# A transformer block on one core: the first FFNs' indirect transfers wait for the one two in front, and all of a scatter goes ahead of the next batch's places

## The chip, the cores and the metric

The kernel runs on one core of a Trainium2 chip. A core has five engines that run their own instruction streams and meet through semaphores: PE (matmul, with a half called PEld that loads weights), DVE (vector), ACT (scalar, activation), POOL (GpSimd) and SP (which here only issues plain DMAs). Plain DMAs are issued by SP; indirect ones, where each of 128 rows goes to or comes from a row number held in SBUF, are issued by POOL. The metric is the device time of one execution in microseconds (us), as the median of several.

## The reference

All is float32; x is 4 batches of 1024 tokens of 128 channels.

```python
x = x + attn_a(layernorm(x))     # gated attention in groups of 32 plus a linear part, 256 inner channels
x = x + ffn(layernorm(x))        # mixture of experts: 8 experts, each token goes to its best 2
x = x + attn_b(layernorm(x))     # 16 heads of 64, softmax over the queries
x = x + ffn(layernorm(x))        # the same experts again

def ffn(x):                      # per batch: T tokens, E = 8, capacity = T / E * 1.25 = 160
    probs = softmax(x @ Wr); topk_probs, topk_experts = top_k(probs, 2)
    pos = place of the token in its expert's queue   # a running count over the tokens
    keep = pos < capacity
    buf[expert, pos] += x * keep                     # scatter to 8 x 160 slots
    y = relu(buf @ W1 + b1) @ W2 + b2                # per expert, hidden 512
    out = sum over k of y[expert, pos] * keep * topk_probs   # gather from the slots
```

## The kernel before

The four batches ("rows" in the code, 0 to 3) pass through attn_a one after the other (`a_tensor`, `a_scalar`, `a_vector`). The FFN's routing of a batch is woven into the row after next or so: while row 2 is worked on, the first FFN batch is scattered, and so on. FFN batches are numbered m = 1, 2, 3 here (the fourth runs inside attn_b). For each m the chain is: logits, choice of two experts on DVE (`choose_vector`), `positions` on PE (a running count by small bfloat16 matmuls with a triangle and with ones), `kept_vector` on DVE, then the "places": arithmetic that turns positions into row numbers of the slot array `xslots` in HBM. For m = 1 and 2 POOL computes the places (`place_gpsimd`), for m = 3 DVE (`place_vector`) and POOL copies the result to `row_s`. Then POOL issues the scatter: 16 indirect transfers (2 choices x 8 tiles of 128 tokens, 512 bytes a row), one after the other in its own stream.

When the transfers go is set by `hold`, a wait on POOL. In the scatters of m = 1 and 2 each transfer or pair waits for an event of the attention on PE (`scatter_in_attention`: a_vproj, a_lktr, a_sq, a_sl, a_kv, a_o, a_out; `scatter_in_next`: a_xproj, a_gproj), and the last three of batch 1's sixteen stand in the row after. The scatter of m = 3 and the gather of batch 1's answers wait, two transfers at a time, for an expert's first product (`beside_expert`, f_h). The landings all count on one semaphore, f_sc, 256 for a scatter. No transfer waits for another.

SP loads the slots back, 640 KB at a time, once the 16 transfers have landed: to `slots_sb` for m = 1, to `slots2` (in `vact`) for m = 2, to `slots3` (in `state`) for m = 3. Between the last two it stores the answers of batch 1 to `yslots`. PE's experts run as `experts_tensor` for m = 1, 2, 3: for each of 8 experts an up product (L412) and a down product (L446), eight blocks each of 1.09 us; `positions` for m = 3 stands behind the third down product of m = 1. The gather of batch 1 (16 indirect transfers, `yg`) feeds DVE's `first_answers_vector`, in four quarters; then come the statistics of the new x, a Newton iteration and the normalized `xhat`, which PE transposes (L498) at the end of `experts_tensor` for m = 3 and which all of attn_b starts from.

Behind that, from about 214 us on, attn_b fills PE, and the later FFN work is done in its side; its indirect transfers are each held for a step of the attention (`paced`).

Of the kernel before, what the change touches and what calls it, by code (L numbers as in the profile page):

```python
# [19 lines left out]
U32 = mybir.dt.uint32  # L20
I32 = mybir.dt.int32
ALU = mybir.AluOpType
# [3 lines left out]
P = 128  # L26
# [23 lines left out]
def bass_hybrid(nc, x, wv, bv, wg, win, wout, bout, cols_a, wr, w1, b1, w2, b2, wqkv, bqk, bvv, wl, bl, out):  # L50
    with ExitStack() as keep:
# [81 lines left out]
        f_plc = sem("f_plc")  # L133
# [133 lines left out]
        def route_norm_scalar(a, k):  # L267
            a.wait_ge(lf_rstd, k + 1)
            if k == 0:
                a.wait_ge(zeroed, ZEROED)  # L270
            elif k == 2:
                a.wait_ge(f_sc, 256)
# [81 lines left out]
        row_s = sb("row_s", [P, 2, T], U32, stack=stage_f)  # L354
        slots_sb = sb("slots_sb", [P, ST, P], stack=stage_f)
# [68 lines left out]
        def experts_tensor(pe, m, beside, residual=None, turned=TR, begun=False, following=None):  # L424

            def up(e):
# [6 lines left out]
                if e == 5 and m == 1:  # L433
                    pe.wait_ge(f_kept, 3)
# [181 lines left out]

        def place_gpsimd(p, step, m):
# [15 lines left out]
            if m > 1:  # L633
                p.wait_ge(f_sc, 256 * (m - 1))
            nc.gpsimd.tensor_copy(row_s[:], skip[:]).then_inc(f_idx, 1)

        def place_vector(v, step, m):
# [11 lines left out]
            nc.vector.tensor_tensor(skip[:], rowf[:], skip[:], ALU.add).then_inc(f_plc, 1)  # L649

        def first_answers_vector(v, step):
# [4 lines left out]
            for q in range(4):  # L656
                v.wait_ge(f_gq[q], 64)
# [8 lines left out]
        def scatter(p, m, tiles):  # L666

            for c in tiles:
                k, t = c // T, c % T
                nc.gpsimd.indirect_dma_start(out=xslots[:, :], out_offset=bass.IndirectOffsetOnAxis(ap=row_s[:, k, t:t + 1], axis=0),  # L670
                                             in_=route_rows(m - 1)[:, t, :], in_offset=None,
                                             bounds_check=B * SLOTS - 1, oob_is_err=False).then_inc(f_sc, 16)

        def scatter_in_attention(p, m, next_row=None):

            r = m + 2
            hold(p, f_idx, m + 1)
            hold(p, a_vproj, 4 * r + 4)
            scatter(p, m, [0])
            hold(p, a_lktr, 2 * r + 2)  # L680
            scatter(p, m, [1])
            hold(p, a_sq, 2 * r + 2)
            scatter(p, m, [2])
            for h in range(2):
                hold(p, a_sl, 2 * r + h + 1)
                scatter(p, m, [3 + h])
            for k in range(2):
                hold(p, a_kv, 4 * r + 2 * k + 1)
                scatter(p, m, [5 + k])
            for k in range(4):  # L690
# [1509 lines left out]
```

## Time and profile before

| | |
|---|---|
| three timed runs | 1462.74, 1464.06, 1464.46 us (median 1464.06) |
| span of the profiled execution, first to last instruction | 1486.9 us |
| the profiled execution's own time beside its span | not reported; it is the span and what lies around it |
| busy: PE, PEld, DVE, ACT, POOL | 1437.6, 1023.7, 1065.3, 917.8, 280.4 us |
| the 16 transfers each of three scatters and one gather | between 79.9 and 201.4 us of the span |

In the rows below a time is in us from the start of the span. In the rows of a timeline the columns are the start, the length, the engine, the line of the kernel, the operation with its operands (written, then read) and how many are merged into the row; the bracket gives the engine's idle time before it and what ended it. "remote" and "another core or an unknown queue" mean that the profile has no instruction to name; "issue" means that it shows nothing that was waited for.

### The profile page before, as it was taken

Reading aid. Unit: us, or ns where it says so; the run is one execution under the profiler, and the core shown is the slowest. Engines: PE = TensorE matmul, PEld = TensorE weight load, DVE = VectorE, ACT = ScalarE, POOL = GpSimd, SP = SyncE. Lnnn points to the kernel's source line nnn. Section 1 sums busy time; section 2 is a strip of 40 time slices with the busy share of each in tenths; the row PEclk is TensorE's granted clock in tenths of the full one; section 3 lists DMA queues with packets and bytes.
Section 4 is the critical chain, followed back from the end, with each engine's and each line's share of the span. In section 5 each row is a group of like instructions: output and inputs, shape, how many; then the busy total and the mean of one; then the engine's idle time right before and its main releaser. Section 6 shows DMA issues by size and latency. Waiting matters only on the chain.

```text
span 1486.9 us, 43341 instructions
## 1 busy us (share of the span) xinstructions
PE 1437.6 (97%) x18426; PEld 1023.7 (69%) x18426; DVE 1065.3 (72%) x2172; ACT 917.8 (62%) x1727; POOL 280.4 (19%) x325
## 2 busy tenths in 40 slices
PE   7999789999999999999999999999999999999996
PEld 6988774566677675667777756577777565677486
DVE  6884037888666678886766788876666887787754
ACT  5774466666666666566666666666666666666542
POOL 4164613013210012130000120400001214000055
PEclk9999999999999999999999999999999999999999
DMA  8501221001110011010000110110101101101002
GB/s 223 196 20 53 68 65 39 22 23 46 30 29 16 16 42 32 23 48 16 17 16 16 41 32 22 35 33 17 30 16 39 32 23 34 34 16 30 1 19 58
DMA packets 44464, 58.30 MB, mean 39 GB/s; under 512 B 8231, under 2 KB 32656, under 8 KB 44144
## 3 DMA queue, kind: packets, MB, share of 16 engines
q1 hardware_dynamic: 35120, 38.27, 9.4%
q0 software_dynamic: 9152, 17.26, 4.4%
q8 instruction: 147, 2.41, 0.7%
q14 instruction: 45, 0.37, 0.1%
HBM read 22.14 MB, written 19.32 MB: 28 GB/s over the span
## 4 chain that ended last, share of the span: by engine, by line
PE 87%; DVE 5%; ACT 3%; issue 2%; another core or an unknown queue 2%; DMA 0%; DVEq 0%; ACTq 0%
PE bank L1153 29%; PE bank L1166 28%; PE bank L1076 6%; PE bank L1081 4%; PE bank L1090 4%; PE bank L412 2%; PE bank L446 2%; PE bank L1308 2%; PE bank L1304 2%; DVE nmx L1188 1%; PE bank L1265 1%; ACT hT L542 1%; PE bank L830 1%; DVE stats L1349 1%
## 5 line engine op out<-in xcount | busy, mean ns | idle before, releaser
L1197 ACT ACTIVATE prob<-bank,nmx 128x1024 f32<-128x1024 f32 x512 | 570.2, 1114 | 420.3 <-DVE nmx L1188 408.5
L1188 DVE TENSOR_REDUCE nmx<-bank 128x1 f32<-128x1024 f32 x512 | 626.2, 1223 | 200.2 <-PE bank L1153 182.3
L1166 PE MATMUL bank<-prob,vsc 64*64 64x512 f32 x4096 | 644.9, 590 | 1.9 <-DVE ctxT L1215 1.4
L1153 PE MATMUL bank<-q,k 64*64 64x512 f32 x2048 | 527.6, 591 | 3.1 <-ACT prob L1197 1.9
L1153 PE MATMUL bank<-q,ks 64*64 64x512 f32 x2048 | 526.3, 590 | 0.0
L1166 PEld LDWEIGHTS bank<-prob,vsc 64*64 64x64 f32 x4096 | 237.3, 133 | 119.4 <-issue 47.1
L1076 PE MATMUL bank<-xT,wqkv_sb 64*64 64x256 f32 (+1 forms) x1560 | 211.7, 434 | 0.0
L1153 PEld LDWEIGHTS bank<-q,ks 64*64 64x64 f32 x2048 | 139.1, 133 | 75.9 <-issue 21.0
L1760 POOL DMA_INDIRECT yg<-yslots,row_ring x64 | 64.9, 1014 | 609.2 <-PE bank L1153 579.8
L1153 PEld LDWEIGHTS bank<-q,k 64*64 64x64 f32 x2048 | 135.3, 133 | 37.6 <-issue 8.6
L1076 PEld LDWEIGHTS bank<-xT,wqkv_sb 64*64 64x64 f32 x1560 | 92.2, 133 | 86.6 <-issue 36.5
L1081 PEld LDWEIGHTS bank<-wqkv_sb,xT 64*64 64x64 f32 x1984 | 105.5, 133 | 34.7 <-issue 16.6
L1090 PEld LDWEIGHTS bank<-wl_sb,ctxT 64*64 64x64 f32 x1984 | 108.1, 133 | 28.2 <-issue 8.9
L1081 PE MATMUL bank<-wqkv_sb,xT 64*64 64x128 f32 x1984 | 118.8, 270 | 0.0
L1090 PE MATMUL bank<-wl_sb,ctxT 64*64 64x128 f32 x1984 | 117.4, 270 | 0.3 <-issue 0.3
L1771 POOL DMA_INDIRECT xslots<-xhat_r,row_s x64 | 62.3, 974 | 206.0 <-PE bank L1153 182.7
L1197 ACT ACTIVATION_READ_ACCUMULATOR prob<-bank,nmx 128x1 f32 x512 | 98.7, 193 | 0.0
L1207 DVE TENSOR_TENSOR vsc<-v,zinv 128x128 f32<-128x128 f32 x256 | 74.8, 292 | 8.8
L1132 DVE TENSOR_TENSOR v<-bank,bvv_sb 128x512 f32<-128x512 f32 x64 | 44.2, 691 | 41.5 <-PE bank L1081 41.2
L542 ACT ACTIVATE hT<-bank,b_sb 128x160 f32<-128x160 f32 x160 | 50.0, 411 | 34.7 <-PE bank L412 20.9
L1304 PE MATMUL bank<-xsT,w_sb 64*64 64x160 f32 x768 | 68.2, 296 | 0.0
L1119 DVE TENSOR_TENSOR xres<-bank,xres 128x512 f32<-128x512 f32 x64 | 44.0, 688 | 23.7 <-PE bank L1090 22.0
(270 smaller groups left out, 1628.6 us busy)
## 6 DMA issues: line engine op xcount, KB each, us to landing
ks<-k SPq DMA_DIRECT2D x62, 256.0 KB
yslots<-slots_sb SPq DMA_DIRECT2D x7, 640.0 KB, 3.6
slots_sb<-xslots SPq DMA_DIRECT2D x5, 640.0 KB, 4.5
xslots<-xhat_r POOLq DMA_DIRECT2D x5, 512.0 KB, 7.0
yslots<-xhat_r POOLq DMA_DIRECT2D x5, 512.0 KB, 12.3
w_sb<-in_w SPq DMA_DIRECT2D x1, 2048.0 KB, 9.2
wqkv_sb<-in_wqkv SPq DMA_DIRECT2D x1, 2048.0 KB, 19.0
xslots<-xhat_r,row_s POOLq DMA_INDIRECT x112
```

What stands on the lines that cost most here:

```text
L542: ins = nc.scalar.activation(hT[:, e % deep(m), c, :], bank[:, UP_BANK[e % deep(m)] + c // 2, cols(c % 2, CAP)], ACT.Relu, bias=b1_sb[:, e ...
L1076: ins = nc.tensor.matmul(bank[rows(h), PJ[0] + t, 0:n], wqkv_sb[rows(r), row, c + h * HD:c + (h + 1) * HD], xT_c[rows(r), k % 2 * HALF + t ...
L1081: ins = nc.tensor.matmul(bank[rows(h), bk, cols(i)], xT_c[rows(r), cols(8 * (k - 4) + 2 * t + h, HD)], wqkv_sb[rows(r), row, WV:WV + P], s ...
L1090: ins = nc.tensor.matmul(bank[rows(h), bk, cols(i)], ctxT[pi % 2][rows(r), cols(8 * k + 2 * t + h, HD)], wl_sb[rows(r), pi % PAIRS, :], st ...
L1153: ins = nc.tensor.matmul(bank[rows(c), SC[h][n], :], kk[r, cols(2 * j + c, HD)], qst[pi % 2][r, cols(n, HALF)], start=True, stop=True)
L1166: ins = nc.tensor.matmul(bank[rows(h), CX[n], :], vsc[s][rows(r), rows(h)], prob[g % 3][h][rows(r), cols(n, HALF)], start=(j == 0 and firs ...
L1188: nc.vector.tensor_reduce(nmx[:, 2 * s + h:2 * s + h + 1], bank[:, SC[h][0]:SC[h][0] + 2, :], mybir.AxisListType.XY, ALU.max, negate=True) ...
L1197: nc.scalar.activation(prob[g % 3][h][:].rearrange("p (n c) -> p n c", c=HALF), bank[:, SC[h][0]:SC[h][0] + 2, :], ACT.Exp, bias=nmx[:, 2 ...
L1207: nc.vector.tensor_tensor(vsc[s][:].rearrange("p (h c) -> p h c", c=HD), vst[pi % 2][:, j, :].rearrange("p (h c) -> p h c", c=HD), zinv[:, ...
L1304: ins = nc.tensor.matmul(bank[rows(h), bk, cols(q, CAP)], w1_sb[rows(r), e, cols(4 * (i % 2) + 2 * q + h, HD)], xsT[rows(r), cols(e, CAP)] ...
L1760: nc.gpsimd.indirect_dma_start(out=yg[:, k, t, :], out_offset=None, in_=yslots[:, :], in_offset=bass.IndirectOffsetOnAxis(ap=row_ring[:, f ...
L1771: nc.gpsimd.indirect_dma_start(out=xslots[:, :], out_offset=bass.IndirectOffsetOnAxis(ap=row_s[:, k, t:t + 1], axis=0), in_=xhat_r[:, t, : ...
```

## The change

- In the three scatters and in the gather of batch 1, every transfer from the third on waits until the one two in front of it has landed. For that the semaphores f_sc and f_gq are split into an even and an odd one for each batch or quarter. The waits on events of the attention and of the experts are gone.
- All sixteen transfers of batch 1 go before the places of batch 2, with the bias of row 3 between the eighth and the ninth; before, three of them stood in the next row. The places of batch 2 go to a buffer of their own, `row_s2`, and no longer wait for the landing of batch 1.
- `positions` for m = 3 stands in front of the experts of m = 1, not behind their third down product. DVE writes the third batch's row numbers to `row_s` itself; POOL's copy is gone.

```diff
@@ semaphores
-        f_plc = sem("f_plc")
...
-        f_sc, f_ld, f_st, f_comb = (sem(n) for n in ("f_sc", "f_ld", "f_st", "f_comb"))
+        f_sc = {m: [sem(f"f_sc{m}{i}") for i in range(2)] for m in (1, 2, 3)}
+        f_ld, f_st, f_comb = (sem(n) for n in ("f_ld", "f_st", "f_comb"))
...
-        f_gq = [sem(f"f_gq{q}") for q in range(4)]
+        f_gq = [[sem(f"f_gq{q}{i}") for i in range(2)] for q in range(4)]
@@ experts_tensor, up(e)
-                if e == 5 and m == 1:
+                if e == 2 and m == 1:
                     pe.wait_ge(f_kept, 3)
@@ first_batch_tensor, beside(e)
-                if e == 3:
-                    positions(pe, 3, POS_F)
                 if e == E - 1:
-                    pe.wait_ge(f_kept, 3)
                     slots_ahead_tensor(pe, 2, slots2, AHEAD[:2])
@@ place_gpsimd
+        def rows_to(m):
+            return row_s2 if m == 2 else row_s
...
-            if m > 1:
-                p.wait_ge(f_sc, 256 * (m - 1))
-            nc.gpsimd.tensor_copy(row_s[:], skip[:]).then_inc(f_idx, 1)
+            nc.gpsimd.tensor_copy(rows_to(m)[:], skip[:]).then_inc(f_idx, 1)
@@ place_vector
-            nc.vector.tensor_tensor(skip[:], rowf[:], skip[:], ALU.add).then_inc(f_plc, 1)
+            for done in f_sc[1]:
+                v.wait_ge(done, 128)
+            nc.vector.tensor_tensor(rows_to(m)[:], rowf[:], skip[:], ALU.add).then_inc(f_idx, 1)
@@ scatter
                 k, t = c // T, c % T
-                nc.gpsimd.indirect_dma_start(out=xslots[:, :], out_offset=bass.IndirectOffsetOnAxis(ap=row_s[:, k, t:t + 1], axis=0),
+                if c > 1:
+                    hold(p, f_sc[m][c % 2], 16 * (c // 2))
+                nc.gpsimd.indirect_dma_start(out=xslots[:, :], out_offset=bass.IndirectOffsetOnAxis(ap=rows_to(m)[:, k, t:t + 1], axis=0),
                                              in_=route_rows(m - 1)[:, t, :], in_offset=None,
-                                             bounds_check=B * SLOTS - 1, oob_is_err=False).then_inc(f_sc, 16)
+                                             bounds_check=B * SLOTS - 1, oob_is_err=False).then_inc(f_sc[m][c % 2], 16)
-        def scatter_in_attention(p, m, next_row=None):
...
-        def scatter_in_next(p, m):
...
-        def beside_expert(p, i):
...
+        FIRST = 8
@@ gather
-                    beside_expert(p, 11 + 2 * q + k)
                     for t in (2 * q, 2 * q + 1):
+                        n = 4 * q + 2 * k + t % 2
+                        if n > 1:
+                            hold(p, f_gq[(n - 2) // 4][n % 2], 16 * ((n - 2) % 4 // 2 + 1))
...
-                                                     bounds_check=B * SLOTS - 1, oob_is_err=False).then_inc(f_gq[q], 16)
+                                                     bounds_check=B * SLOTS - 1, oob_is_err=False).then_inc(f_gq[q][t % 2], 16)
@@ the block of gpsimd
             place_gpsimd(p, step, 1)
-            scatter_in_attention(p, 1, 3)
-            scatter_in_next(p, 1)
+            hold(p, f_idx, 2)
+            scatter(p, 1, range(FIRST))
+            bias_gpsimd(p, 3)
+            scatter(p, 1, range(FIRST, 2 * T))
             place_gpsimd(p, step, 2)
-            scatter_in_attention(p, 2)
-            scatter(p, 2, [13, 14, 15])
-            p.wait_ge(f_plc, 1)
-            p.wait_ge(f_sc, 256 * 2)
-            nc.gpsimd.tensor_copy(row_s[:], skip[:]).then_inc(f_idx, 1)
+            hold(p, f_idx, 3)
+            scatter(p, 2, range(2 * T))
             hold(p, f_idx, 4)
-            for i in range(8):
-                beside_expert(p, 3 + i)
-                scatter(p, 3, [2 * i, 2 * i + 1])
+            scatter(p, 3, range(2 * T))
             gather(p, step, 1, 0)
@@ the block of tensor
             pe.wait_ge(f_sub, 4)
+            positions(pe, 3, POS_F)
             experts_tensor(pe, 1, first_batch_tensor(pe), (a_res, 10), following=slots2)
```

Beside these, the waits on f_sc in `route_norm_scalar`, `load_slots`, `f_norm_vector` and SP's block become waits on the two semaphores of the batch (128 each).

The POOL stream around the end of the second scatter and the start of the third, before (row_s and row_s2 are the row numbers, xhat_r and xhat_r1 the rows sent):

```order
L670 DMA xslots<-xhat_r1,row_s 5120x128 [waits a_o] x4
L670 DMA xslots<-xhat_r1,row_s 5120x128 [waits a_out] x2
L670 DMA xslots<-xhat_r1,row_s 5120x128 x3
L2065 CAST row_s<-skip 128x16 [waits f_sc,f_plc]
L670 DMA xslots<-xhat_r,row_s 5120x128 [waits f_idx,f_h]
L670 DMA xslots<-xhat_r,row_s 5120x128
```

and now:

```order
L675 DMA xslots<-xhat_r1,row_s2 5120x128 [waits f_sc20]
L675 DMA xslots<-xhat_r1,row_s2 5120x128 [waits f_sc21]
L675 DMA xslots<-xhat_r,row_s 5120x128 [waits f_idx]
L675 DMA xslots<-xhat_r,row_s 5120x128
L675 DMA xslots<-xhat_r,row_s 5120x128 [waits f_sc30]
L675 DMA xslots<-xhat_r,row_s 5120x128 [waits f_sc31]
```

The waits on PE's events (a_o, a_out, f_h) have given way to waits on landings of the same scatter, and POOL's copy between the two scatters is gone.

The PE stream at the end of row 3 and the start of the experts, before (chosen holds the choice, xsT the slots, hT the hidden values):

```order
L852 MATMUL bank<-wout_sb,gateT 128x128 x15
L412 MATMUL bank<-xsT,w1_sb 128x160 [waits f_xs,f_sub,load_f]
L412 MATMUL bank<-xsT,w1_sb 128x160 [waits a_res]
L446 MATMUL bank<-hT,w2_sb 128x160 [waits f_ya,f_ha]
L379 MATMUL bank<-chosen,before 128x64 [waits f_m]
L412 MATMUL bank<-xsT,w1_sb 128x160 [waits f_ha,f_kept]
```

and now:

```order
L824 MATMUL bank<-wout_sb,gateT 128x128 x15
L381 MATMUL bank<-chosen,before 128x64 [waits f_m,f_sub,load_f]
L383 MATMUL bank<-chosen,ones 128x56
L414 MATMUL bank<-xsT,w1_sb 128x160 [waits f_xs]
L414 MATMUL bank<-xsT,w1_sb 128x160 [waits f_kept,a_res]
```

The count of positions has moved ahead of the first expert, and the wait for f_kept from the sixth expert's up product to the third's.

## Rows read from the trace of the kernel before

**Rows 1.** The page: who holds the chain that ended last

```profile
PE 87%; DVE 5%; ACT 3%; issue 2%; another core or an unknown queue 2%; DMA 0%; DVEq 0%; ACTq 0%
```

**Rows 2.** The chain of waits, 108 to 215 us: start, length, what

```profile
119.87 6.31 another core or an unknown queue
...
154.43 3.92 another core or an unknown queue
...
161.37 2.67 another core or an unknown queue
...
179.47 3.62 another core or an unknown queue
...
184.43 3.54 issue
```

**Rows 3.** Timeline of ACT and of PE, 110 to 225 us

```profile
126.20 1.08 ACT L331 ACTIVATE xT_r<-bank 128x512 f32<-128x512 f32 x2 [6.33 <-remote]
...
120.23 1.04 PE L313 MATMUL bank<-ident,xhat_r 128*128 128x128 f32 x8
...
127.43 2.64 PE L370 MATMUL bank<-wr_sb,xT_r 128*128 128x8 f32 x16 [0.25 <-ACT xT_r L331]
```

**Rows 4.** Timeline of POOL, 0 to 330 us

```profile
79.94 1.12 POOL L670 DMA_INDIRECT xslots<-xhat_r,row_s  x1 [1.04 <-issue]
...
148.55 0.20 POOL L2065 CAST row_s<-skip 128x16 uint32<-128x16 f32 x1 [5.54 <-DVE skip L649]
149.70 0.98 POOL L670 DMA_INDIRECT xslots<-xhat_r,row_s  x1 [0.95 <-POOL row_s L2065]
150.99 0.97 POOL L670 DMA_INDIRECT xslots<-xhat_r,row_s  x1 [0.30 <-issue]
...
171.39 0.97 POOL L670 DMA_INDIRECT xslots<-xhat_r,row_s  x1 [0.30 <-issue]
...
178.49 1.00 POOL L721 DMA_INDIRECT yg<-yslots,row_g  x1 [0.30 <-issue]
...
200.44 1.00 POOL L721 DMA_INDIRECT yg<-yslots,row_g  x1 [0.30 <-issue]
```

**Rows 5.** Windows: stretch, its length, busy time, then the granted clock (PEclk)

```profile
128.50:135.20 6.70, 6.70 (x33) 6.70 (x33) 3.78 (x17) 1.81 (x5) 1.69 (x2) 0.50 0.10 32
...
186.50:193.20 6.70, 5.23 (x20) 5.23 (x21) 1.49 (x6) 2.64 (x7) 0.79 (x1) 0.50 0.08 20
400.00:560.00 160.00, 160.00 (x2322) 115.34 (x2318) 110.21 (x169) 102.97 (x191) 14.93 (x15) 1.00 0.10 25
```

**Rows 6.** Timeline of ACT near the end

```profile
1475.17 0.88 ACT L1868 ACTIVATE answers<-bank,slot_owner 128x128 fp32r<-128x128 f32 x3 [9.69 <-remote]
```

**Rows 7.** Timeline of PE in row 2

```profile
89.03 0.82 PE L313 MATMUL bank<-ident,xhat_r 128*128 128x128 f32 x6
...
94.52 1.85 PE L370 MATMUL bank<-wr_sb,xT_r 128*128 128x8 f32 x16
```

**Rows 8.** Timeline of DVE: it takes up the gathered rows, then xhat

```profile
181.09 1.26 DVE L654 SCALAR_TENSOR_TENSOR xres<-yg,wtok_ring,xres 128x128 f32<-128x128 f32 x4 [32.61 <-DMA yg<-yslots,row_g]
...
203.42 1.26 DVE L654 SCALAR_TENSOR_TENSOR xres<-yg,wtok_ring,xres 128x128 f32<-128x128 f32 x4 [3.62 <-DMA yg<-yslots,row_g]
...
208.54 2.14 DVE L1374 TENSOR_SCALAR xhat<-xres,meanvar,rstd 128x128 f32<-128x128 f32 x8
```

**Rows 9.** SP's queue: the store of answers and the load of state

```profile
167.20 0.36 SPq L732 DMA_DIRECT2D yslots<-slots_sb  x1
173.63 0.36 SPq L1995 DMA_DIRECT2D state<-xslots  x1
```

**Rows 10.** Timeline of PE: the experts' wait for kept; the transposes of xhat

```profile
146.67 1.35 PE L412 MATMUL bank<-xsT,w_sb 128*128 128x160 f32 x8 [0.45 <-DVE tmp L615]
...
211.95 1.04 PE L498 MATMUL bank<-ident,xhat 128*128 128x128 f32 x8
```

**Rows 11.** Groups of POOL's instructions by line: the scatters inside attn_b

```profile
L1771 POOL DMA_INDIRECT xslots<-xhat_r,row_s x64 | 62.3, 974 | 206.0 <-PE bank L1153 182.7 <-issue 23.2
```

More of the change, by code:

```diff
@@ L271, in route_norm_scalar @@
             elif k == 2:
-                a.wait_ge(f_sc, 256)
+                for done in f_sc[1]:
+                    a.wait_ge(done, 128)
             for half in range(2):
@@ L354, in bass_hybrid @@
         row_s = sb("row_s", [P, 2, T], U32, stack=stage_f)
+        row_s2 = sb("row_s2", [P, 2, T], U32, stack=stage_f)
         slots_sb = sb("slots_sb", [P, ST, P], stack=stage_f)
@@ L648, in place_vector @@
                                               kept[:].rearrange("p k t -> p (k t)"), ALU.mult))
-            nc.vector.tensor_tensor(skip[:], rowf[:], skip[:], ALU.add).then_inc(f_plc, 1)
+            for done in f_sc[1]:
+                v.wait_ge(done, 128)
+            nc.vector.tensor_tensor(rows_to(m)[:], rowf[:], skip[:], ALU.add).then_inc(f_idx, 1)
         def first_answers_vector(v, step):
@@ L656, in first_answers_vector @@
             for q in range(4):
-                v.wait_ge(f_gq[q], 64)
+                for done in f_gq[q]:
+                    v.wait_ge(done, 32)
                 for k in range(2):
@@ L669, in scatter @@
                 k, t = c // T, c % T
-                nc.gpsimd.indirect_dma_start(out=xslots[:, :], out_offset=bass.IndirectOffsetOnAxis(ap=row_s[:, k, t:t + 1], axis=0),
+                if c > 1:
+                    hold(p, f_sc[m][c % 2], 16 * (c // 2))
+                nc.gpsimd.indirect_dma_start(out=xslots[:, :], out_offset=bass.IndirectOffsetOnAxis(ap=rows_to(m)[:, k, t:t + 1], axis=0),
                                              in_=route_rows(m - 1)[:, t, :], in_offset=None,
-                                             bounds_check=B * SLOTS - 1, oob_is_err=False).then_inc(f_sc, 16)
-        def scatter_in_attention(p, m, next_row=None):
[L676 to L690, printed above, removed]
-                hold(p, a_o, 4 * r + k + 1)
-                scatter(p, m, [7 + k])
-                if k == 1 and next_row is not None:
-                    bias_gpsimd(p, next_row)
-            for h in range(2):
-                hold(p, a_out, 2 * r + h + 1)
-                scatter(p, m, [11 + h])
-        def scatter_in_next(p, m):
-            r = m + 3
-            hold(p, a_xproj, 2 * r + 2)
-            scatter(p, m, [13])
-            for k in range(2):
-                hold(p, a_gproj, 4 * r + 2 * k + 2)
-                scatter(p, m, [14 + k])
-        def beside_expert(p, i):
-            hold(p, f_h, E + i + 1)
+                                             bounds_check=B * SLOTS - 1, oob_is_err=False).then_inc(f_sc[m][c % 2], 16)
+        FIRST = 8
         def gather(p, step, m, b):
@@ L1415, in f_norm_vector @@
                 else:
-                    v.wait_ge(f_sc, 256 * (B - 1))
+                    for done in f_sc[B - 1]:
+                        v.wait_ge(done, 128)
                 xhat_vector(v, c0, fb, xhat_r, piece - 5, g_xhat)
@@ L1992, in _ @@
                     store_slots(sp, 1, 0)
-                hold(sp, f_sc, 256 * m)
+                for done in f_sc[m]:
+                    hold(sp, done, 128)
                 hold(sp, f_ld, 16 * m)
```

3 lines of the change are left out of this document (2 added, 1 removed).

## The prediction

> **What bounds the kernel now.** I read the page first: the chain that ended last is 87% PE, so most of the 1,486.9 us is matmul time that nothing in this change touches [rows 1]. The change lies between 79.9 and 204 us, on POOL's indirect transfers, so I went on to the chain of waits in 108 to 215 us. It is PE and ACT work, broken by five stretches in which the chain can name no instruction: 6.31, 3.92, 2.67, 3.62 and 3.54 us, 20.1 us in all [rows 2]. I call them freezes. They are not waits for data. ACT's copy of xT_r starts at 126.20 after 6.33 us of idle, although the transposes that it reads began at 120.23 and take 1.04 us [rows 3]. Then I set POOL's rows beside them [rows 4]: every freeze falls into a run of indirect transfers issued back to back, one each 1.28 us (scatter) or 1.30 us (gather). After them PE runs at half clock: granted 0.50 from 128.5 to 135.2 and from 186.5 to 193.2 [rows 5], which is 1.2 of 2.4 GHz, each time after PE had had gaps.
>
> Are the freezes there when nobody records? The span is 1,486.9 us; what lies around it only adds to it; the three timed runs have a median of 1,464.06 us. So the recorded execution is at least 22.8 us longer than an ordinary one. From 214 to 1,400 us there is no room for that: PE works nearly without a gap at full clock. What I can take out as freeze is about 17 us up to 212 us (worked out below) and some 8 us at the end, where the same kind of freeze holds ACT for a good part of 9.69 us [rows 6]. 1,486.9 - 25 = 1,462, next to the median. The likeliest reading is that the timed runs hardly have these freezes. So my sum is made on a clock of the profile without them, and carried over to the median as a difference.
>
> **That clock.** Row 2 of the attention turns its first block at 89.03, row 3 at 120.23, 31.20 later. In row 2 the logits start at 94.52, behind 0.87 us of transposes that row 3 lacks; so row 3's belong at 124.85 and stand at 127.43: +2.6. The 6.7 us at half clock that follow leave 3.3 us of work undone: 5.9 us in all [rows 3, 5, 7]. Next, xsT is late by about 2.9 us at 158.37 and yT by 2.7 at 164.06 [rows 2]: 11.5 us by the store at 167.20, which belongs at 155.7 [rows 9]. From there to the transposes of xhat PE has 30 blocks of eight matmuls at 1.09 (32.7), 2.2 of transposes and some 2 of short waits: 37, so PE is done at 192.7, not 211.95 [rows 10].
>
> **The path before.** The third FFN's scatter starts at 149.70 - 5.9 = 143.8. Sixteen at 1.28: the last starts at 162.9 and ends at 163.9. The load of state that waits for it comes 2.24 after its start, at 165.1, and makes PE wait less than a us (193.5) [rows 9]. The copy of row_g and 0.95 of start-up put the first gather at 165.0; with 15 x 1.30 the last starts at 184.5. DVE takes it up 2.98 later and ends xhat 7.26 after that (203.42 to 208.54 + 2.14) [rows 4, 8]: 194.8. So POOL's chain already ends about a us behind PE. That is the stage's bound.
>
> **The change part by part.**
> 1. *The wait for the one two in front.* Nothing but the next transfers stands behind it on POOL. Three kinds of row price it. A scatter is seen landed 2.24 us after its start (171.39 to the load at 173.63). A gather is seen landed 2.60 us after the start of the fourth of the first quarter (178.49 to 181.09) and 2.98 after that of the last (200.44 to 203.42) [rows 4, 8, 9]. And from the end of what an indirect transfer waited for to its own start there are 0.95 us (row_s at 148.55 + 0.20, transfer at 149.70) [rows 4]. In the present stream that 0.95 lies beside the transfer before; behind a landing it lies bare. So a pair takes 2.24 + 0.95 = 3.2 us, or 1.60 each, for scatters and 2.60 + 0.95 = 3.55, or 1.78 each, for gathers. Ends: nothing (1.28 and 1.30 kept, if most of the 0.95 still overlaps), and 1.97 for gathers (2.98 throughout). I take 1.60 and 1.78, as the rows are from this very stage.
> 2. *Scatter before places.* Batch 1: eight transfers from 79.94 [rows 4], the last at 90.8; then the bias of row 3, which waits for ACT's xhat of that row and so ends near 94.2; eight more from 94.4, the last ends at 106.3, some 2.6 us before the present end. The places of batch 2 take 4.7 us and end at 111.0; POOL began them without idle before, and f_kept, which comes from DVE at the head of row 3, is there by then as well. Batch 2's sixteen from 112.0: the last starts at 135.7. Row 3 no longer has its holds (a_o, a_out), so POOL is not late through PE any more, only through its own pace.
> 3. *Positions in front of the experts, DVE writes row_s itself.* PE ends the output products at 131.4 (137.3 - 5.9), so positions end near 131.9 and DVE's residual, which stands ahead of kept, near 132.6; then 0.5, and the 2.1 us from f_kept (146.6) to row_s (148.75): f_idx at 135.2, against 142.9 before (148.75 - 5.9) [rows 4, 10]. It removes a PE wait of 0.45 us [rows 10] and POOL's copy. The eight small matmuls (0.35 us) only move. The third expert's up waits for f_kept, which comes about when PE gets there.
> 4. *Batch 3 and the gather.* POOL is free at 137.0, so most of the 7.7 us won by part 3 is lost to the pace of batch 2. Sixteen at 1.60: the last starts at 160.6; copy and start-up: first gather at 162.8 (the store has landed near 159.7); the last starts 1.3 + 24.9 later, at 188.9; + 2.98 + 7.26 = 199.0. The load of state now comes early enough and gives PE its 0.8 back, unused.
> 5. *Semaphores split by parity, more holds on SP, DVE, ACT:* waits long met; cost nothing.
>
> Sum: 199.0 - 194.8 = +4.2 us at the transposes of xhat, on which all of the attention behind depends, and which nothing later gives back (PE is the bound from there on). PE would stand still for some 5 us there; the half clock behind earlier gaps [rows 5] could add 1 to 3 us, shorter landings without the recorder take as much off. I say +4: 1,468 us.
>
> The Trainium skill, DMA: Bandwidth & Descriptors, section "Anatomy of one DMA — SWDGE (gpsimd) path", puts about 2.0 us of fixed cost on a transfer, most of it completion, while many descriptors can be emitted before that costs anything. This speaks against the change: what was hidden behind the next issue becomes the pace. My rows have 2.24 to 2.98, so the trace agrees in kind and is higher in size. By the page's 2.0 the pace would be an estimated 1.48 for both, the last gather would start near 182, and POOL would be no later than before; that is the second rival's result.
>
> **The rivals.**
> - *The freezes are real in every execution and the pace ends them.* The price is what the profile shows: xhat's transposes move from 211.95 to about 199 to 200, -12 to -13 us, so 1,451. It decides from the point at which more than about 7 us of the 17 exist in a timed run. For it: they are large, all lie in back-to-back runs, and the far looser stream of the attention behind (64 scatters with 206 us of idle before them [rows 11]) shows none. Against it: 1,464 leaves no room for them. A remainder of 5 to 10 us would give 1,455 to 1,461.
> - *The pace costs less than the start gains.* With 1.50 and 1.70 the same sum ends at 195.9 (+1.1); with 1.28 and 1.30 batch 3 starts at 136.2, xhat is done by 187, and PE's 192.7 is the bound (-2). So 1,462 to 1,466. For it: all latencies were read while the recorder ran; against it: they come from two kinds of transfer and three places that agree within 0.8 us.
> - *The change doesn't do what it says:* two in flight is what a landing of 2.25 at a step of 1.28 keeps anyway, so real freezes would stay, beside the cost of the pace: 1,466 to 1,470.
>
> **How the numbers follow.** The kernel's own runs differ by 1.7 us; about 0.2% (2.9 us) is what can be told from no change. Forecast (+2.9 to +8) 0.43; pace for nothing (-2.9 to +2.9) 0.28; freezes real and ended 0.25, half of it with the full gain; real and kept 0.04. Slower 0.46, same 0.30, faster 0.24. The forecast's own range is 1,466 to 1,472; the high end is gathers at 1.97 (+7) and a little half clock. Downwards I reach to 1,453, so that only the full gain is left out.
>
> **What would show it.** In the changed kernel's profile: scatters 1.5 to 1.65 us apart and gathers 1.7 to 1.85 (1.3 would prove the second rival's pace, over 1.9 the high end); the last gather near 189 us; DVE's last sum 2.6 to 3.0 us behind it; PE waiting at the transposes of xhat for DVE, not for slots. The freezes may well be gone from the record, and its span some 12 us shorter: that alone doesn't show a gain in the timed runs, and I would be right only if they still come out longer. I am wrong if the timed runs follow the record.

## The result and the profile after

The changed kernel took 1479.32 us in the median of four runs (1477.55 to 1480.85), the kernel before 1463.4 us beside it (1461.79 to 1464.46): a ratio of 1.0108 [1.0094, 1.0123]. It is 15.9 us slower; +4 was forecast, with 1,472 us as the high end. The direction was right, the size wrong by a factor of four.

The profiled execution of the changed kernel took 1478.24 us with a span of 1476.2, so 2.0 us lie around the span. The page's line on the chain, and PE's longest waits between 60 and 230 us (line <- what ended the wait: us in total, times, longest), answer to [rows 1, 10]:

```profile
PE 85%; issue 4%; DMA 3%; POOL 3%; DVE 3%; ACT 1%; POOLq 0%; DVEq 0%; ACTq 0%
```

```profile
PE bank L497 <- DVE xhat L1346: 11.4, 1, 11.4
PE bank L403 <- DMA state<-xslots: 4.8, 1, 4.8
```

POOL and DMA now have a share of the chain, and PE stands still for 11.4 us before the transposes of xhat. The load of state, which was to come early enough, makes it wait 4.8. Timeline of POOL from the end of batch 2's scatter into the gather, answering to [rows 4]:

```profile
137.99 0.97 POOL L675 DMA_INDIRECT xslots<-xhat_r,row_s  x1 [0.57 <-issue]
139.26 0.97 POOL L675 DMA_INDIRECT xslots<-xhat_r,row_s  x1 [0.31 <-issue]
140.54 0.97 POOL L675 DMA_INDIRECT xslots<-xhat_r,row_s  x1 [0.30 <-issue]
142.43 0.97 POOL L675 DMA_INDIRECT xslots<-xhat_r,row_s  x1 [0.91 <-DMA xslots<-xhat_r,row_s]
147.17 0.97 POOL L675 DMA_INDIRECT xslots<-xhat_r,row_s  x1 [3.77 <-DMA xslots<-xhat_r,row_s]
148.45 0.98 POOL L675 DMA_INDIRECT xslots<-xhat_r,row_s  x1 [0.30 <-issue]
...
166.56 0.98 POOL L675 DMA_INDIRECT xslots<-xhat_r,row_s  x1 [0.31 <-issue]
...
168.67 1.08 POOL L692 DMA_INDIRECT yg<-yslots,row_g  x1 [0.93 <-POOL row_g L683]
170.06 1.01 POOL L692 DMA_INDIRECT yg<-yslots,row_g  x1 [0.30 <-issue]
174.32 1.00 POOL L692 DMA_INDIRECT yg<-yslots,row_g  x1 [3.25 <-DMA yg<-yslots,row_g]
...
177.76 1.00 POOL L692 DMA_INDIRECT yg<-yslots,row_g  x1 [1.14 <-DMA yg<-yslots,row_g]
...
186.48 1.00 POOL L692 DMA_INDIRECT yg<-yslots,row_g  x1 [2.89 <-DMA yg<-yslots,row_g]
...
198.93 0.99 POOL L692 DMA_INDIRECT yg<-yslots,row_g  x1 [0.61 <-issue]
```

An undisturbed pair of scatters costs 1.28 + 1.80 = 3.08 us, a pair of gathers from 1.30 + 2.1 = 3.4 up to 3.66 (3.5 in the mean of four). That is 1.54 and 1.70 to 1.83 a transfer, where the forecast has 1.60 and 1.78: the price of an undisturbed pair was right. Between such pairs stand waits of 3.77, 3.25 and 2.89 us. The chain of waits has the landings behind them (start of the transfer, time until its landing released POOL, what), and the timeline of SP's queue shows what moved beside them:

```profile
113.02 3.76 DMA xslots<-xhat_r,row_s
...
140.54 5.79 DMA xslots<-xhat_r,row_s
...
154.88 3.43 DMA xslots<-xhat_r,row_s
...
168.67 4.81 DMA yg<-yslots,row_g
...
174.32 2.60 DMA yg<-yslots,row_g
177.76 2.70 DMA yg<-yslots,row_g
181.30 4.34 DMA yg<-yslots,row_g
```

```profile
140.24 0.38 SPq L1969 DMA_DIRECT2D vact<-xslots  x1
154.32 0.36 SPq L704 DMA_DIRECT2D yslots<-slots_sb  x1
168.85 0.36 SPq L1969 DMA_DIRECT2D state<-xslots  x1
181.64 0.36 SPq L704 DMA_DIRECT2D yslots<-slots_sb  x1
```

Four of the landings are late, 5.8 and 3.4 us for scatters, whose median here is 2.2, and 4.8 and 4.3 for gathers, against 2.6 and 2.7 between them. Each belongs to a transfer issued within 0.6 us of a plain transfer of 640 KB. A fifth late landing, 3.76 us from 113.02 on, makes POOL wait 2.28 us at 117.62 with no plain transfer beside it: the load of slots_sb had been issued at 107.47 and had landed by 111.9.

The wait on PE ends with DVE's xhat, from its timeline:

```profile
207.22 2.14 DVE L1346 TENSOR_SCALAR xhat<-xres,meanvar,rstd 128x128 f32<-128x128 f32 x8
```

Behind that long wait PE works at half clock (granted 0.50). In a table of windows (stretch, length, busy time of PE, PEld, DVE, ACT and POOL, then the granted clock):

```profile
208.40:214.00 5.60, 5.52 (x22) 4.10 (x24) 2.22 (x6) 2.66 (x5) 0.00 (x0) 0.50 0.00 0
```

For comparison a second record of the kernel before is wanted, because its first has the freezes. It was taken later (below) with a span of 1462.4 us, and it has no freeze. Its timelines of POOL, DVE and PE answer to [rows 4, 8, 10]:

```profile
82.30 1.12 POOL L670 DMA_INDIRECT xslots<-xhat_r,row_s  x1 [1.04 <-issue]
...
164.43 0.97 POOL L670 DMA_INDIRECT xslots<-xhat_r,row_s  x1 [0.30 <-issue]
...
186.24 1.00 POOL L721 DMA_INDIRECT yg<-yslots,row_g  x1 [0.30 <-issue]
```

```profile
194.33 2.14 DVE L1374 TENSOR_SCALAR xhat<-xres,meanvar,rstd 128x128 f32<-128x128 f32 x8
```

```profile
195.59 2.05 PE L498 MATMUL bank<-ident,xhat 128*128 128x128 f32 x8 [2.21 <-DVE xhat L1374]
```

The first scatter starts at 80.1 us in some executions and near 82 in others, of the old kernel and the new alike; so the stage is best measured from there. From the first scatter's start to the end of xhat the kernel before takes 196.47 - 82.30 = 114.2 us (forecast: 194.8 - 79.94 = 114.9). The changed kernel takes 209.36 - 80.17 = 129.2 (forecast 119.1). That is +15.0, and the median time rose by 15.9. The two recorded executions themselves differ by 14.0 us: 15.0 in this stage, 2.1 less ahead of the first scatter (80.17 for 82.30), and some 1.4 more right behind xhat. Nothing behind gives anything back.

### The profile page after: what moved, and what is told of

Its sections match the earlier page's. It is cut to its first block, busy times and chain, and to the rows that moved or that the text cites. A ratio compares the mean times of both kernels' runs of the same rounds, so it can differ in the third digit from the quotient of the medians.

```text
span 1476.2 us, 43358 instructions
## 1 busy us (share of the span) xinstructions
PE 1428.9 (97%) x18426; PEld 1026.2 (70%) x18426; DVE 1068.6 (72%) x2172; ACT 918.7 (62%) x1727; POOL 280.6 (19%) x324
## 4 chain that ended last, share of the span: by engine, by line
PE 85%; issue 4%; DMA 3%; POOL 3%; DVE 3%; ACT 1%; POOLq 0%; DVEq 0%; ACTq 0%
PE bank L1125 30%; PE bank L1138 29%; PE bank L1048 6%; PE bank L1053 4%; PE bank L1062 3%; PE bank L1280 2%; POOL xslots L675 2%; PE bank L1276 2%; DMA yg<-yslots,row_g 2%; PE bank L1237 1%; DMA xslots<-xhat_r,row_s 1%; PE bank L414 1%; PE bank L448 1%; DVE nmx L1160 1%; PE bank L1909 1%
## 5 line engine op out<-in xcount | busy, mean ns | idle before, releaser
L1138 PEld LDWEIGHTS bank<-prob,vsc 64*64 64x64 f32 x4096 | 240.4, 133 | 116.5 <-issue 41.6
L1280 PE MATMUL bank<-hT,w_sb 64*64 64x160 f32 x768 | 60.2, 296 | 0.0
```

What stands on the lines that cost most here:

```text
L1138: ins = nc.tensor.matmul(bank[rows(h), CX[n], :], vsc[s][rows(r), rows(h)], prob[g % 3][h][rows(r), cols(n, HALF)], start=(j == 0 and firs ...
L1280: ins = nc.tensor.matmul(bank[rows(h), bk, 0:CAP], w2_sb[rows(r), i, q, rows(h)], hT[rows(r), i % 2, q, :], start=first and q == 0, stop=n ...
```

## The experiments

"Free" below is the changed kernel without the waits for landings, so only the new order. Ratios are to the kernel before, run beside each.

**1. The pace taken apart.** Free leaves out both of these lines, gather free only the second, scatter free only the first:

```diff
-                if c > 1:
-                    hold(p, f_sc[m][c % 2], 16 * (c // 2))
...
-                        if n > 1:
-                            hold(p, f_gq[(n - 2) // 4][n % 2], 16 * ((n - 2) % 4 // 2 + 1))
```

> The changed kernel without the waits for landings (three scatters and the gather issue freely); order, positions and semaphores as changed. Theory (the pace is the whole cost, and it is the bound through POOL's chain): 1461 to 1464 us, 0 to 2 us under the kernel before, since scatter 3 starts earlier and PE becomes the bound. Rival 1 (the new order costs by itself): stays above 1470. Rival 2 (recorded freezes are real in timed runs): its record shows freezes again and the timed run is then longer than the changed kernel's 1479. The theory expects the freezes back in the record, span 1480 or more, with a timed run near 1463.

> The changed kernel with the pace in the scatters alone; the gather issues freely. Theory: the gather takes 15 x 1.30 instead of 30.3 us, so xhat is ready some 10.5 us earlier (near 198.5): 1467 to 1470 us, still some 5 us over before, for the load of state comes late (PE waits 4.8 us for it). Rival (the order costs): as the changed kernel, 1479, less little.

> The changed kernel with the pace in the gather alone; scatters issue freely. Theory: scatter 3 starts near 136 and ends by 156, so the gather starts when the store has landed, 9 to 10 us earlier: 1468 to 1471 us. Together with the other half (gather free) the two savings need not add up, as PE is the bound behind some 192 us. Rival (the order costs): 1479.

Measured: free 1458.5 us, 0.9969 [0.9957, 0.9981]; pace in the scatters only 1466.95, 1.0024 [1.0015, 1.0033]; pace in the gather only 1468.0, 1.0037 [1.0024, 1.0051]. So the new order alone is 4.7 us faster than before, where I expected 0 to 2, and the pace costs 20.8 us on top (21.6 when both were run again side by side): 8.4 for scatters and 9.5 for gathers alone. Why the medians of the two don't add up to the whole is not shown. PE's slack in the free version, which either half uses up first, is small: xhat is ready at 188.8 and PE comes to it at 190.13. The records have it larger for each half: the stretch from the first scatter's start to the last gather's is 98.2 us in the free version, 109.9 and 109.3 with the pace in the scatters or the gather, and 118.8 with both, and the recorded executions took 11.6, 11.0 and 21.9 us more than free's. Of free, the timeline of POOL, and of PE at the transposes:

```profile
130.84 0.98 POOL L673 DMA_INDIRECT xslots<-xhat_r,row_s  x1 [0.30 <-issue]
135.46 0.98 POOL L673 DMA_INDIRECT xslots<-xhat_r,row_s  x1 [3.65 <-DVE row_s L651]
...
154.73 0.98 POOL L673 DMA_INDIRECT xslots<-xhat_r,row_s  x1 [0.30 <-issue]
158.75 1.09 POOL L688 DMA_INDIRECT yg<-yslots,row_g  x1 [2.83 <-DMA yslots<-slots_sb]
...
178.38 0.99 POOL L688 DMA_INDIRECT yg<-yslots,row_g  x1 [0.30 <-issue]
```

```profile
190.13 1.04 PE L497 MATMUL bank<-ident,xhat 128*128 128x128 f32 x8
```

POOL is led by data (row_s at 135.46, the store at 158.75), and PE reaches the transposes without a wait. My expectation that the freezes would be back in this record fell: it shows none, although every scatter and the gather are issued back to back once their data is there. That a back-to-back stream is enough for them is refuted.

The free version's record has late landings too, although nothing waits for them. Its gathers issued at 174.48, 175.78 and 177.08 land after 4.5, 4.8 and 3.7 us, beside the store of batch 2's answers (issued at 174.85); so the pace doesn't make these landings late, it only waits for them. But three of its scatters, at 111.51, 124.41 and 140.60, land after 3.7, 3.9 and 3.9 us with no plain transfer under way. Plain transfers are therefore not the only source of late landings; the other one is open.

**2. How far in front.** Three kernels wait for the landing of the one directly in front, three in front and four in front (the last two with four semaphores instead of two). The wait of the scatters in the first of them:

```diff
-                if c > 1:
-                    hold(p, f_sc[m][c % 2], 16 * (c // 2))
+                if c > 0:
+                    hold(p, f_sc[m][(c - 1) % 2], 16 * ((c + 1) // 2))
```

> The changed kernel, but each indirect transfer waits for the landing of the one directly in front. My theory: a transfer in this form costs its landing plus the bare start-up behind a wait: scatters 2.3 + 0.9 = 3.2 us apart (1.6 in the changed kernel), gathers 2.7 + 0.9 = 3.6 to 3.8 (1.85 to 1.9). 48 scatters x 1.55 + 16 gathers x 1.85 is about 104 us more before xhat, nothing of it hidden: 1,565 to 1,600 us. Rival, the start-up lies beside the landing in front: 2.3 and 2.7 us apart, so 0.75 x 48 + 0.85 x 16 = 50 us more, 1,525 to 1,535. Rival, the cost of the pace sits in what the holds do to other engines and not in the landings: far below 1,520.

> The changed kernel, but each transfer waits for the landing of the one three in front. My theory (a landing and 0.9 us of start-up have to fit into n steps of issue): 2.3 + 0.9 = 3.2 is under 3 x 1.28 = 3.84, and 2.7 + 0.9 = 3.6 under 3.90, so the pace costs nothing but beside the plain transfers of 640 KB, about 1 to 3 us at each of the four in the way, of which 3.7 us are hidden behind PE: 1,458 to 1,462. Rival, any wait for a landing costs its start-up of 0.9 us bare: 0.3 us per transfer and 1,468 to 1,474.

> The changed kernel, but every transfer waits for the one four in front instead of two (four semaphores for each scatter). Theory: four transfers cover 4 x 1.28 = 5.1 us, more than a landing of 2.2 to 3 plus 0.9, so the wait binds only beside a plain 640 KB transfer (landings up to 5 us): within 2 us of the kernel with no waits, 1462 to 1466. Rival (a wait on POOL costs by itself, landed or not): near 1479. If recorded freezes come from a deep queue, they are here as in the kernel with no waits.

Measured: one 1568.91 us, 1.0722 [1.0706, 1.0739]; (two: 1479.32); three 1460.05, 0.9976 [0.9966, 0.9987]; four 1457.84, 0.9959 [0.9945, 0.9972]. "Four" came out 4 us below its range of 1,462 to 1,466, which was built on too slow a forecast for free, but within the 2 us of free that the expectation named; "one" and "three" lie in theirs. With "one", POOL's timeline shows the whole price of a landing with the start-up bare:

```profile
154.42 0.98 POOL L675 DMA_INDIRECT xslots<-xhat_r,row_s  x1 [1.97 <-DMA xslots<-xhat_r,row_s]
157.37 0.97 POOL L675 DMA_INDIRECT xslots<-xhat_r,row_s  x1 [1.98 <-DMA xslots<-xhat_r,row_s]
...
281.94 0.99 POOL L692 DMA_INDIRECT yg<-yslots,row_g  x1 [2.66 <-DMA yg<-yslots,row_g]
285.63 0.99 POOL L692 DMA_INDIRECT yg<-yslots,row_g  x1 [2.69 <-DMA yg<-yslots,row_g]
```

Undisturbed, that is 2.95 to 3.1 us a scatter and 3.4 to 3.7 a gather. So the form of the cost holds: landing plus start-up has to fit into n steps of issue. Two steps (2.56 to 2.60) are too short. Three (3.84, 3.90) are long enough except at late landings (3.6 to 5.8 us in that record), which lengthen the stage by 4.6 us over free but the time by only 1.5. Four cost nothing. Four in front and free can't be told apart; they are the best versions run, some 5 us below the kernel before.

**3. The pace in the old order.** The kernel before with the same two waits for landings, its holds on PE and ACT kept.

> The kernel before with its order of work, but every scatter and gather waits for the landing of the one two in front. My theory: the pace costs the same in either order wherever transfers stood back to back, that is in batch 3's scatter and in the gather: about 0.35 x 16 + 1.9 for the plain store beside it = 7.5 us, and the 9.5 us that the gather's pace alone cost; so about 17 us over the kernel before less 0 to 3 us of slack: 1,476 to 1,481 us, as slow as the changed kernel. In its record the freezes are gone, if it is the stream back to back that makes them there; they stay, if the holds on PE and ACT make them. Rival, the pace costs so much only in the new order, in which all 48 scatters stand in one row: 1,466 to 1,471.

Measured: 1481.56 us, 1.0127 [1.0112, 1.0143], 0.6 us above the range. The pace costs about 18 us in the old order too, although batches 1 and 2 are led by the attention there. The rival (only the new order suffers) fell. Its record has no freeze; that decides nothing, as the second record of the kernel before has none either (experiment 6).

**4. What the new order gains.** Free, with `positions` back beside the fourth expert:

```diff
+                if e == 3:
+                    positions(pe, 3, POS_F)
...
-            positions(pe, 3, POS_F)
             experts_tensor(pe, 1, first_batch_tensor(pe), (a_res, 10), following=slots2)
```

> The version without any wait for a landing (1,458.5 us), but with positions of batch 3 back beside the fourth expert, as in the kernel before: of the new order only 'all of a scatter ahead of the next places, no holds on PE and ACT' is left. My theory: the gain of 4.7 us over the kernel before comes from the earlier row_s of batch 3 alone; without it batch 3's scatter starts near 143.8 instead of 135.5, the last gather near 184.5 instead of 178.4, and POOL's chain sets xhat again near 194.5: 1,462 to 1,464 us. Rival, the gain comes from the holds that are gone (POOL no longer led by PE and ACT): 1,458 to 1,460.

Measured: 1463.56 us, 1.0002 [0.9993, 1.0011]. Within the noise the whole gain is the earlier row_s: here batch 3's scatter starts 62.8 us behind the first one of all (144.67 - 81.84) instead of 55.3 (135.46 - 80.19), and PE waits 2.3 us for xhat again. Scattering ahead and dropping the holds gain nothing by themselves.

**5. Plain transfers and the pace.** One kernel takes a plain transfer out of the gather: SP's store of batch 2's answers waits until the gather has landed. Four add some, from x to a scratch tensor of its size that nobody reads, without and with the pace; the eight go one behind the other. The first half of the eight:

```diff
+            hold(sp, a_lktr, 10)
+            for n in range(4):
+                hold(sp, f_extra, 16 * n)
+                sp.dma_start(extra[:, :].rearrange("(i p) c -> p i c", p=P),
+                             x[0:SLOTS, :].rearrange("(i p) c -> p i c", p=P)).then_inc(f_extra, 16)
             hold(sp, a_res, 2 * (B + 1))
```

> The changed kernel, but SP's store of batch 2's answers (640 KB, issued at 181.6 us in the changed kernel, in the middle of the gather) waits until the gather has landed. My theory: the wait of 2.89 us at 186.48 becomes a usual one of 1.1, the one behind it loses 0.4: 2 us less, 1,476.5 to 1,478.5. Rival, the load of state just before (landing near 173) sets these waits: no change, 1,479 to 1,480.

> The changed kernel with four plain transfers more of 640 KB (rows of x into a scratch tensor that nobody reads), two in batch 2's scatter and two in the gather. My theory: an indirect transfer beside a plain one of 640 KB lands 2 to 3 us later, and with the pace POOL stands still for it, each time: 4 x 2 to 3 us, 1,486 to 1,492 us, with four more idle times of 2 us and over in front of POOL's transfers in the record. Rival, the long waits of the changed kernel only happen to lie beside the plain transfers: 1,479 to 1,481.

> The same four plain transfers more, in the version without any wait for a landing (1,458.5 us without them). My theory: without the pace a late landing is nobody's business except of the last transfer; POOL issues on at 1.28 and 1.30: 1,458 to 1,461 us. Rival, the plain transfers slow the indirect stream itself (shared queues or bandwidth), with or without a pace: 1,464 to 1,470.

Measured: store later 1477.63 us, 1.0095 [1.0081, 1.0109]: 1.7 us less than the changed kernel, as expected, but with intervals that overlap. Its record is clearer: behind the load of state no gather lands later than 3.1 us, where the changed kernel has 4.3 and 4.2, and the gather is 1.7 us shorter (28.58 for 30.26). Its scatters have two late landings without a plain transfer beside them, at 113.17 and 124.46. Four more with the pace 1482.12, 1.0128 [1.0113, 1.0144]: +2.8, where I expected 8 to 12, with intervals that overlap again. Four more, free: 1456.76, 0.9955 [0.9942, 0.9969], no cost and 1.2 us below my range. The chain of waits of the paced one shows two of its four additional transfers in the gather at 188.65 and 197.01:

```profile
182.79 5.02 DMA yg<-yslots,row_g
188.65 4.11 DMA yg<-yslots,row_g
193.59 2.58 DMA yg<-yslots,row_g
197.01 4.21 DMA yg<-yslots,row_g
```

The gathers beside the two land 1.5 us late each, not 2 to 3. In the scatters the load of vact cost POOL less than before (1.64 us of wait for 3.77); why is not shown. To settle it, eight more:

> The changed kernel with eight plain transfers of 640 KB more, one behind the other: four from the start of row 4's attention on (beside batch 2's scatter), four behind the store in the gather. Each takes some 4.8 us, so for about 20 us in either place every indirect transfer has a plain one beside it. My theory: a landing beside one takes 3.5 to 5 us, a pair of indirect transfers so about 4.7 instead of 3.1 (scatter) and 5 to 5.7 instead of 3.4 (gather); 4 pairs in either place: +6 and +8, less 2 us for waits that the changed kernel has there already: 1,489 to 1,494. Rival, only the first transfer beside a plain one is late (0.7 us of time for each plain transfer, as four of them cost 2.8 us): 1,483 to 1,486. Rival, plain transfers have nothing to do with it: 1,479 to 1,480.

> The same eight plain transfers more in the version without any wait for a landing. My theory: POOL issues on at 1.28 and 1.30, and late landings matter only at the end of a batch: 1,456 to 1,461. Rival, eight of them take so much from the indirect stream that this version slows as well: 1,464 or over.

Everything in this pair's sitting (the runs that were taken together) came out slower than before: the kernel before took 1486.15 us beside it (nine runs, 1482.88 to 1487.27), the paced kernel 1496.92 (1.0079 [1.0065, 1.0092]) and the free one 1512.41 (1.0173 [1.0158, 1.0189]). The section on the hardware comes back to that. Both were run again, now beside the changed and the free kernel without additions, with the kernel before at 1462.39:

> The changed kernel itself, once more. The kernel before took 1,463 us beside all the experiments but the last pair; beside those it took 1,486, which is what its first record shows, freezes and all. So the freezes can be in ordinary executions too, for as long as a condition lasts that no row names. If the kernel before takes 1,463 beside this one: 1,479 us, freezes in neither. If it takes 1,486: by the theory that only an unpaced stream freezes 1,479 to 1,482, so the change is the faster one there; by the rival that the condition slows any kernel alike 1,500 to 1,503.

> The version without any wait for a landing once more. If the kernel before takes 1,463 beside it: 1,458. If it takes 1,486: by the theory that only an unpaced stream freezes at least 1,482; by the rival that the freezes need something else 1,458.

> The changed kernel with eight plain transfers more, again, now beside the changed kernel itself. If the kernel before takes 1,463: my theory (each landing beside a plain transfer is late and POOL waits for it) says 1,489 to 1,494, the rival (0.7 us for each plain transfer) 1,483 to 1,486. If it takes 1,486: 1,497 as in the last pair, 12 to 18 us above the changed kernel by my theory.

> The version without waits with eight plain transfers more, again. If the kernel before takes 1,463: by my theory no slower than without them, 1,457 to 1,461. If it takes 1,486: 1,512 as in the last pair, with long stretches in which every engine stands still.

| | no addition | eight more | difference |
|---|---|---|---|
| with the pace | 1479.9, 1.0123 [1.0107, 1.0140] | 1486.75, 1.0159 [1.0141, 1.0177] | +6.9 us |
| free | 1458.26, 0.9970 [0.9959, 0.9982] | 1460.1, 0.9981 [0.9971, 0.9990] | +1.8 us |

In the records the stretch from the first scatter to the last gather goes from 117.4 to 131.3 us with the pace and from 98.07 to 98.15 free. The 13.9 us are too much, as the recorded execution with the eight took 1491.16, 4.4 above the median of its kernel, and the one without 1475.58, 4.3 below. In the timeline of POOL with the pace the waits stand where the additions are:

```profile
204.27 0.99 POOL L694 DMA_INDIRECT yg<-yslots,row_g  x1 [2.70 <-DMA yg<-yslots,row_g]
...
209.24 0.99 POOL L694 DMA_INDIRECT yg<-yslots,row_g  x1 [2.67 <-DMA yg<-yslots,row_g]
...
213.68 1.00 POOL L694 DMA_INDIRECT yg<-yslots,row_g  x1 [2.15 <-DMA yg<-yslots,row_g]
```

So plain transfers do make landings late, and the pace turns that into time. By the timed runs it is 0.9 us for each, between the two forecasts: just above the rival's range (1,483 to 1,486) and below mine (1,489 to 1,494), so neither price is confirmed. The intervals of the two paced kernels just part, those of the free ones overlap.

**6. A second record of the kernel before.**

> The kernel before once more, for a second record. If the freezes come with the recorder whenever this program is recorded, the span is again 1,480 us or over with stretches of 2.5 to 6 us in which every engine stands still; if they were a chance of that one execution, the span is 1,458 to 1,465, 2 to 4 us below the timed runs, as in every other kernel here, with PE's last 'down' before xhat near 192 us. Rival to my reading of the timed runs: they contain some freezes as well, then a record without them has a span below 1,456.

Measured: 1464.22 us with a span of 1462.4. The recorded execution is as long as the unrecorded ones beside it (1460.11 to 1464.46), so recording does not bring the freezes: the first record, with a span of 1486.9 us, was an execution that did have them.

## Why the prediction was right in direction and wrong in size

- **The freezes.** Right for the timed runs: they lack them, and the clock without freezes holds (114.9 us forecast from the first scatter to xhat, 114.2 in the second record; PE waits 2.2 us for xhat there, about 1 was forecast). Wrong was the reason, "when nobody records".
- **Part 1, the pace: the step that failed.** I priced a landing as a constant, 2.24 us (scatter) and 2.60 (gather), from moments at which nothing else moved. For undisturbed pairs that was right: 3.08 and 3.4 to 3.7 us for 3.2 and 3.55. What the sum puts at nothing are the late landings: in the changed kernel the sixteen transfers of batch 2, of batch 3 and of the gather take 24.97, 27.30 and 30.26 us from first to last start; at 8 short and 7 long steps without a late landing they would take 22.8, 22.8 and 25.1. That is 2.1 + 4.5 + 5.2 = 11.8 us (by the mean pair of gathers, 3.5 us, the last term is 4.4 and the sum 11.0). The forecast had 23.7 (112.0 to 135.7), 23.6 (137.0 to 160.6) and 26.1 (162.8 to 188.9) for the same three, so it was short by 9.1; another 1.0 us lies in batch 1, its places and DVE's end. That is all of the 10.1 us by which xhat came later than forecast. All four plain transfers were in the trace of before, two of them in [rows 9]; I used them only as work that waits for POOL, not as traffic beside it.
- **Whose the 11.8 us are** is shown in part. The gather's 5.2 us are: all of its late landings lie beside plain ones, the store's went away with the store (experiment 5), and added transfers made new ones. Batch 3's 4.5 us lie beside plain transfers as well, but a scatter at 140.60 of the free version lands after 3.9 us without one, so the 5.8 us from 140.54 on need not be the load's alone. The 2.1 us of batch 2, about 1.5 of them from the late landing at 113.02, have no plain transfer beside them, and their cause is open.
- **What part 1 had right.** Without the late landings xhat would have come 3.2 to 4.0 us later than before (129.2 - 114.2, less 11.8 or 11.0), near the 4.2 of the sum. So the part that was priced was priced well, and the larger part of the rise comes from what the sum lacked. The Trainium skill (DMA: Bandwidth & Descriptors, section "Anatomy of one DMA — SWDGE (gpsimd) path") has about 2.0 us of fixed cost; with the waits for the one directly in front the trace agrees for scatters (3.0 less 0.9 us of start-up) and is higher for gathers (3.5 less 0.9).
- **Parts 2 and 3.** Right in kind. Batch 2 starts 32.9 us after the first scatter (forecast 32.1). The earlier positions are worth 5.1 us if the pace doesn't take them (free against late positions: 1458.5 and 1463.56), and the pace took all of it: POOL came to batch 3 at 139.26, when row_s was already there (134.67).
- **Part 4.** "The load of state now comes early enough" was wrong: the load waits for all of batch 3's landings and is issued at 168.85, not near 162.8, and PE waits 4.8 us. That is not on the path, since POOL is later still.
- **Part 5.** The split semaphores cost nothing that can be seen: four in front has twice as many and is as fast as free, and free with late positions, which has the split, is as fast as the kernel before.
- **Half clock.** 1 to 3 us were kept for it. From the transposes to DVE's first maximum in attn_b it is 10.8 us in the changed kernel, 9.4 in the second record of before and 7.7 in the free version: 1.4 us of the 15.9.
- **Rivals.** Freezes real and ended: false in the timed runs of the comparison, but not unreal (last section). The pace costs less than the start gains: false, 1,479 and not 1,462 to 1,466; with the wait for the one three in front (1460.05) or four (1457.84) it is true. The change doesn't do what it says: the pace does hold POOL back, and in the one paced record taken under the freezes the paced stage has none (last section).

## What to carry to other kernels

A wait for the landing n transfers in front is free only if landing plus start-up fits into n steps of issue. Price it with the late landings that occur, not only with the usual one: here even the usual 2.3 + 0.9 us did not fit into 2 x 1.28, and with the late ones the pace cost about 20 us; with three steps (3.84) only late landings were felt (1.5 us of time), with four (5.1) nothing was. Before pricing such a wait, lay the timeline of every other queue beside it: eight more plain transfers of 640 KB cost the unpaced stream 1.8 us, within the noise, and the paced one 6.9. And if a record's span is longer than the timed runs by more than what usually lies around a span, take a second record before explaining it.

## What the runs showed of the hardware that was not expected

The freezes (POOL's stream runs on through most of them; the other engines stand still or crawl) are part of timed executions without a recorder's doing, under some condition that no row names. It held for all runs of one sitting of the six: the kernel before took 1486.15 us in nine runs, as in its first record (span 1486.9), and in the five other sittings 1462.4 to 1463.9, among them one on the same chip. The chain of waits of the free kernel with eight plain transfers more, in that sitting (times as above):

```profile
124.34 13.24 another core or an unknown queue
...
160.89 3.84 another core or an unknown queue
...
168.72 5.92 another core or an unknown queue
...
1491.39 8.67 another core or an unknown queue
```

From the first scatter to the last gather this kernel took 129.3 us there and 98.15 in an ordinary sitting. The paced one took 126.8 there, 131.3 (in its longest execution) ordinarily; its chain has such a piece only in the tail, where transfers aren't paced, and in the paced stage PE's only waits over 2 us are for state (6.7 us) and for xhat (14.7):

```profile
1474.14 8.67 another core or an unknown queue
```

So the condition costs the paced kernel some 10 us (1496.92 against 1486.75), the kernel before 24 and the free one 52 (1512.41 against 1460.1). The first rival's mechanism is probably real: in the one paced kernel run under the condition the freezes stay out of the stage that is paced. One record shows it, and why it should be so is not shown. What the changed kernel itself takes under the condition was not run. An estimate is 1496.92 - 6.9 = 1,490 us, from the difference that eight transfers make ordinarily; that would be no gain over 1,486 either. What brings the condition about stays open (the chip alone doesn't: of two sittings on the same chip one has it), and so does what free and four in front take under it without the additions.
